# Local attention's product with the values: stationary tiles of 32 queries in place of 64

## The reference

```python
sc = jnp.einsum('bhnid,bhnjd->bhnij', Qb, Kw) / np.sqrt(D)     # block n: 64 queries, 128 keys
sc = jnp.where(mask[None, None], sc, -jnp.inf)
p = jax.nn.softmax(sc, axis=-1)
out = jnp.einsum('bhnij,bhnjd->bhnid', p, Vw)
...
lp = jax.nn.softmax(lsc, axis=-1)                              # 512 queries, 64 latents
rem = jnp.einsum('bhsn,bhnd->bhsd', lp, GV)
...
out = (gl * local + gr * rem) @ w_out
```

## Time and profile before

| | us |
|---|---|
| median of 3 runs | 3002.09 (2997.60 to 3002.82) |
| the profiled execution | 3003.33, its span 3001.5 |
| TensorE (PE) matmuls busy | 2668.5 |
| weight loads (PEld) busy | 1793.9 |
| VectorE (DVE) busy | 1795.5 |
| ScalarE (ACT) busy | 1091.1 |
| line 828, bdV: 7680 matmuls | 263.6 busy |
| line 828, bdL: 2048 matmuls | 88.4 busy |

### The profile page before, as it was taken

How to read it: one execution, slowest core, us unless ns; L and a number is a source line. 1 busy time by engine, 2 the same in 40 slices (tenths; PEclk the granted TensorE clock), 3 DMA queues, 4 the chain that set the end, 5 groups by cost and what they waited for, 6 DMA issues and landing times. The chain is left out here.

```text
span 3001.5 us, 83138 instructions
## 1 busy us (share of the span) xinstructions
PE 2668.5 (89%) x32904; PEld 1793.9 (60%) x32904; DVE 1795.5 (60%) x5503; ACT 1091.1 (36%) x1898; POOL 752.9 (25%) x998
## 2 busy tenths in 40 slices
PE   2899899899999899899899994299999999999998
PEld 1566666666666566566666663166656565666666
DVE  4556556556556556566566556775767667675720
ACT  0343343343343343433333431143333434343343
POOL 1011111121121121121121100134444453434543
PEclk9999999999999999999999998599999999999999
DMA  2000000010010010010000001001020211101020
GB/s 71 11 23 24 17 24 23 17 28 18 17 28 18 18 29 16 19 28 16 21 26 16 23 9 45 15 29 59 30 64 28 65 46 49 64 28 61 30 67 29
DMA packets 51568, 93.71 MB, mean 31 GB/s; under 512 B 7980, under 2 KB 36728, under 8 KB 51096
## 3 DMA queue, kind: packets, MB, share of 16 engines
q0 software_dynamic: 18432, 50.36, 5.9%
q1 hardware_dynamic: 32792, 38.52, 3.9%
HBM read 55.29 MB, written 33.55 MB: 30 GB/s over the span
## 5 line engine op out<-in xcount | busy, mean ns | idle before, releaser
L985 PE MATMUL S_ps<-hT,w 128*128 128x512 f32 x1024 | 478.4, 614 | 15.1 <-ACT hT L694 12.1
L998 PE MATMUL O_ps<-w,hid 128*128 128x256 f32 x2048 | 460.3, 379 | 0.0
L496 POOL DMA_INDIRECT rows<-in_tok_table,idx_now x128 | 129.4, 1011 | 1171.5 <-PE M_ps L883 928.0
L998 PEld LDWEIGHTS O_ps<-w,hid 128*128 128x128 f32 x2048 | 383.0, 190 | 62.5 <-issue 15.3
L1096 DVE TENSOR_REDUCE mxL<-S_ps 128x16 f32<-128x2048 f32 x128 | 293.0, 2289 | 155.8 <-PE S_ps L804 155.8
L632 ACT ACTIVATE PT<-S_ps 128x2048 f32<-128x2048 f32 x128 | 240.3, 1878 | 279.0 <-PE S_ps L772 279.0
L705 ACT ACTIVATE hid<-S_ps,b 128x512 f32<-128x512 f32 x256 | 175.3, 687 | 425.4 <-PE S_ps L985 408.5
L985 PEld LDWEIGHTS S_ps<-hT,w 128*128 128x128 f32 x1024 | 190.0, 194 | 223.5 <-issue 212.1
L828 PEld LDWEIGHTS O_ps<-bdV,PT 128*64 128x64 f32 x7680 | 249.2, 138 | 53.4 <-issue 47.5
L665 ACT ACTIVATE bdV<-M_ps 64x256 f32<-64x256 f32 x256 | 98.8, 386 | 490.7 <-PE M_ps L900 489.2
L828 PE MATMUL O_ps<-bdV,PT 128*64 128x34 f32 x7680 | 263.6, 225 | 1.9 <-DVE loc L1112 1.9
(11 more groups left out here) (237 smaller groups left out, 4248.5 us busy)
## 6 DMA issues: line engine op xcount, KB each, us to landing
h_rows<-h SPq DMA_DIRECT2D x64, 256.0 KB, 2.1
w<-in_w SPq DMA_DIRECT2D x16, 1024.0 KB, 5.9
rows<-in_tok_table,idx_now POOLq DMA_INDIRECT x128, 3.5
out_rows<-orow,idx_cur POOLq DMA_INDIRECT x128, 2.4
PT<-in_tables SPq DMA_DIRECT2D x1, 1024.0 KB
b<-in_b SPq DMA_DIRECT2D x8, 128.0 KB, 4.9
hrow<-h_rows,idx_next POOLq DMA_INDIRECT x64
hrow<-h_rows,idx_cur POOLq DMA_INDIRECT x64
```

The source lines that it names most:

```text
L985: mm = nc.tensor.matmul(S_ps[:, m % 2, 0:GT * P], w1[:, c, m * P:(m + 1) * P], hT[g % 2][:, c, :], start=c == 0, stop=c == KC - 1)
L998: mm = nc.tensor.matmul(O_ps[:, q % 2, 0:D], hid[:, m, q * P:(q + 1) * P], w2[:, m, :], start=m == 0, stop=m == FC - 1)
```

## The change

Each matmul of 64 stationary columns becomes two of 32. The loop over a runs over four groups of 32 queries, each of which writes its own 32 partitions of `O_ps`; the moving operand, the order of the head pairs, the start and stop flags and the semaphores are as before. Between the new constant and this loop every line number is one higher in the changed file, from the loop on two higher.

```diff
+QW = 32
...
             for p in range(NP + LP):
                 for back in (1, 0):
-                    for a in range(2):
-                        x = 2 * t + a
+                    for a in range(NG):
+
+                        x, q = 2 * t + a // 2, QW * (a % 2)
                         if p >= NP and back or x < back:
                             continue
                         if p < NP:
-                            weights, vals = PT[:, p, x - back, W * back:W * (back + 1)], bdV[par][:, x - back, p, :, :]
+                            weights, vals = PT[:, p, x - back, W * back + q:W * back + q + QW], bdV[par][:, x - back, p, :, :]
                         else:
-                            weights, vals = PL[:, p - NP, W * x:W * (x + 1)], bdL[par][:, p - NP, :, :]
-                        mm = nc.tensor.matmul(O_ps[W * a:W * (a + 1), t % 2, 2 * OW * p:2 * OW * (p + 1)], weights,
+                            weights, vals = PL[:, p - NP, W * x + q:W * x + q + QW], bdL[par][:, p - NP, :, :]
+                        mm = nc.tensor.matmul(O_ps[QW * a:QW * (a + 1), t % 2, 2 * OW * p:2 * OW * (p + 1)], weights,
                                               vals.rearrange("p j d -> p (j d)"), start=back == 1 or x == 0 or p >= NP,
                                               stop=back == 0)
```

## The result

The changed kernel takes **3071.62 us** (median of 4 runs, 3066.80 to 3080.51), the one before 3002.45 (4 runs). The ratio is 1.0236, its 95% interval 1.0208 to 1.0264: slower by 69 us, where 2962 was forecast and the range ended at 3008.

The account below looks back on a forecast made before the run. TensorE was taken as the attention part's bound, VectorE's maxima hiding most value stages. First value stage 32 us, fourth 2.6, jumps 3.6, last sequence 2: 40 us less, forecast 2962 us, range 2944 to 3008.

Parts of the forecast that it names:

- What bounds the kernel: Attention part: TensorE bounds; of four value stages (line 828) the first gains 1.0 us a sequence, the others hide behind VectorE.
- One column group: Value line: a 32-column group takes 32 ns a pair instead of 58.3, 40 pairs 1.28 us; first stage 1.05 us shorter.
- the rival of two groups: Value line: four column groups share the rate of two, 15.5 ns a pair; no gain, about 3000 us, chance 0.09.
- Starting them: Value line: TensorE can start pairs every 10 ns in the first value stage, 8 ns in the others.
- the first rival: Value line: pairs cannot start faster than every 25 ns across the engine; 154 us slower, 3156 us, chance 0.13.
- Instructions arrive too late: TensorE's code supply, 16 KB transfers: late requests cost up to 4.2 us a sequence, near 3110 us, chance 0.05.
- The clock: Attention part: granted clock stays at 1.00 through the new waits; behind jumps it could fall more often, a few us.
- The sum: First value stage 32 us, fourth 2.6, loop jumps 3.6, last sequence 2; together 40 us less, giving 2962 us.

Follow-up runs that it names:

- O0 gave 19: Kernel before the change, with 32-column tiles only in the first of each sequence's four value-product stages: 2982.19 us, ratio 0.9940.
- with the code elsewhere: Kernel before the change, 32-column tiles only in the first value-product stage, plus 64 pairs at the program start: 2993.33 us, ratio 0.9970.
- With O0 and O3: Kernel before the change, with 32-column tiles only in the first and fourth value-product stages: 2977.61 us unshifted, ratio 0.9918.
- O1 to O3 alone: Kernel before the change, with 32-column tiles in the second to fourth value-product stages, 64 in the first: 3058.20 us, ratio 1.0196.
- With O0 and O3 and the shift of 32 pairs: Kernel before the change, 32-column tiles only in first and fourth value-product stages, plus 16 matmuls at the program start: 2974.40 us, ratio 0.9914.

## Why the prediction was wrong

- *What bounds the kernel* (O0 on the path, O1 to O3 under VectorE's reductions): right, though O0 gave 19 or, with the code elsewhere, 8 us, and not 32. With O0 and O3 the wait moved to ML. O1 to O3 alone gave nothing; that run has stalls in them and cannot tell what they would give without. But in the sequence of the changed kernel above, S8 starts at 1109.01, after a wait of 1.04 us, 0.14 us behind the end of this reduction, as forecast:

```profile
1106.58 2.29 DVE L1098 TENSOR_REDUCE mxL<-S_ps 128x16 f32<-128x2048 f32 x1 [0.64 <-PE S_ps L805]
```

- *One column group*: right. Forecast 8 ns a pair and 1.4 to 1.5 us for O0 to S5, measured 8.7 and 1.60. Four groups do work at once; the rival of two groups (15.5 ns) is out.
- *Starting them*: right. 128 pairs pass in 1.30 us at full clock, so the first rival, 25 ns as a limit of the whole engine, is out; the 25 ns of the earlier trace rows were those of 32 pairs in one array tile. Against the rule of the Trainium skill on about 60 cycles for each matmul, in "TensorEngine Tiling (Array Packing)", section Performance Considerations, the trace has 8.7 ns for a pair across four tiles; the 4 ns between tiles of the Trainium skill's page "TensorE: Matmul & The Clock Gate", Part 3, is the nearer one.
- *Instructions arrive too late* was named, priced near 3110 and given 0.05. It is what happened. The step that failed is the sentence "one occupies an engine for 1.17 us, so the rate suffices". It took the length of a transfer for the distance between two. The distance is 3.47 to 3.75 us, three times that, and O0 was to use up one in 1.28. The sum therefore put the supply at nothing, and 142 us of issue waits stood in its place. The next sentence but one, that 260 instructions in 3.8 us show no stall, was true and was read the wrong way: it bounds the distance only from above, and the kernel was within 7% of it.
- *The clock* was costed at "a few us": the new waits for VectorE hardly lowered it, but with the stalls it was lower, and that was some 37 us, more than O0 was to bring. Before, the clock falls six times in the attention part, each time behind a jump; in the changed kernel it falls 25 times, with no idle time above 2.7 us outside the jumps. With O0 and O3 and the shift of 32 pairs, where VectorE's `mp` is waited for 24 times but hardly a stall is left, it falls 8 times.
- *The sum*: -40 us was forecast. The busy time of the value line fell by 101.8; in its place came 142 us of issue waits (118.5 + 16.1 + 4.7 + 2.7) and 49 us more busy time on the other lines of the account, through the clock and the interruptions. The waits for VectorE absorbed 21 of that and the jumps 2, and 65 us are left.

## What to carry to other kernels

Splitting a matmul into smaller tiles buys array time with instructions; before it is done, count how many instructions the engine uses up in its densest stretch and compare with what its code queue has ever delivered, by the distance of two transfers and not by the length of one. Make the split only in the stage that is on the path: here one stage of four had the gain, and the other three had the cost. When idle time is ended by "issue" at the same place of the program in every pass, move the code by half a transfer: if the stalls move with it, it is the supply.

## What the runs showed of the hardware

- TensorE's code came in transfers of 16 KB, each 256 instructions. In dense code they followed one another at 3.47 to 3.75 us when the burst between took 2.04 us at half clock, at 3.74 us in the case shown with a burst of 1.30 us at full clock, and at 7.3 us once beside two loads of 1 MB. The transfer itself was 0.88 to 1.35 us of that.
- Four column groups of 128 rows by 32 columns with float32 operands ran at 8.7 ns for a pair of load and matmul, more than three times the rate of two groups of 64 columns (29.1 ns), within a burst.
- A shift of the program by 64 or 128 instructions changed its time by 1.1%, with the same work but for the few matmuls that make the shift (2974.40 against 3007.22 and 3008.27 us).
